# A block of feed-forward, attention and feed-forward on one core: the score banks are taken in an order fixed per head, out of turn at two units

## The chip, the cores and the metric

One Trainium2 chip, of which the kernel uses one core. The metric is the device time of one execution in microseconds (us), here the median of the runs.

## The reference, cut to what matters

```python
x = x + 0.5 * ffn(layernorm(x))
x = x + attention(layernorm(x))
x = x + 0.5 * ffn(layernorm(x))

def attention(x):                      # x: (2, 2048, 512), 16 heads of 32
    q, k, v = (proj(w_q), proj(w_k), proj(w_v))
    scores = einsum('bhqd,bhkd->bhqk', q, k) * SCALE
    probs = softmax(scores, axis=-1)
    attn = einsum('bhqk,bhkd->bhqd', probs, v)
    return einsum('bsd,ed->bse', attn, w_o)
```

All of it is float32. The change lies in the middle line alone, in `scores` and the exponential of the softmax.

## The kernel before

The program has three stages: the first feed-forward with the projections for q, k and v, the attention, and the output projection with the second feed-forward. The attention runs over 32 heads (16 heads of each of the two batch items, `NH`), numbered H = 0 to 31. A head has 16 key tiles of 128 keys (`KT`), and each key tile meets 4 chunks of 512 queries (`QC`), so a head has 64 units (`UNITS`) of 128 keys by 512 queries. Unit i of a head is chunk i mod 4 of key tile i div 4.

For each unit TensorE makes one score matmul (`scores`, line 903) into one of three PSUM banks (`s_ps`, `SR` = 3). ScalarE takes the exponential out of that bank (`scalar_tile`, line 891) and counts it in the semaphore `exp_done`. Behind each score matmul TensorE makes one matmul of the next head's maxima (`maxima`, line 907) into one of four other banks, which VectorE reduces (line 836). So that no score overwrites a bank that ScalarE has still to read, TensorE waits ahead of every score matmul for the exponential of the unit that used the bank last. The banks are taken in rotation over all units of all heads, so this is always the unit three before, and 64 units being no multiple of three, the rotation starts on another bank in each head.

TensorE's order is written out by hand in `tensor_group`. A group is two key tiles, so eight units: score, maximum, score, maximum, sixteen matmuls in all, and then the sixteen matmuls with v of the two key tiles of the group before (`out_tile`, line 934). Groups are numbered u = 0 to 7 here. After group 3 come the matmuls of the row sums (lines 950 and 958), after group 6 a transpose (line 926) of the next head's maxima, which VectorE and two DMAs carry into `att_q` ahead of the next head's first score. ScalarE also copies the output of the head before out of PSUM, between the exponentials of units 9 and 10 (line 286), and the row sums before unit 32. In the last two heads the output projection is worked in: TensorE's line 382, GpSimd's 353 and 357, ScalarE's 366. GpSimd and DMAs add up the exponentials of a head; eight tiles of them (`prob`, `PR` = 8) are kept, and ScalarE waits for the oldest to come free (`tile_free`).

Of the kernel before, what the change touches and what calls it, by code (L numbers as in the profile page):

```python
# [7 lines left out]
ACT = mybir.ActivationFunctionType  # L8
AX = mybir.AxisListType

P = 128
# [5 lines left out]
CH = 512  # L17
# [4 lines left out]
QC = SEQ // CH  # L22
# [13 lines left out]
def f32(ap):  # L36
    return ap.bitcast(F32)
# [142 lines left out]
class Stream:  # L180
# [11 lines left out]
    def load(self, sp, N, src):  # L192
        sp.dma_start(self.x[N % 2][:], chunk(src, N % NCH)).then_inc(self.loaded[N % 2], 16)
# [455 lines left out]
            st.norm.tensor(pe, self.PE_AT[t], N + 1)  # L649


NB = 3
KQ, KM = 3 * HD, 3 * HD + 2
LEAD, G = 4, 2
NG = KT // G
PR = 8
SR, MR = 3, 4
UNITS = KT * QC
AHEAD = LEAD * QC
SUMS_AFTER = 3  # L660
SUMS_AT, TURN_AT = QC * G * (SUMS_AFTER + 1), QC * 7 * G
SLOTS = UNITS + 2
CHAINS = 2
# [5 lines left out]
def sums_after(H):  # L669

    return SUMS_AFTER if H < NH - 1 else SUMS_AFTER - 1
# [6 lines left out]
def slot(p):  # L678

    return p + (p >= SUMS_AT) + (p >= TURN_AT)  # L680


SUMS_SLOT, TURN_SLOT = SUMS_AT, TURN_AT + 1
AT_SLOT = {slot(p): p for p in range(UNITS)}


def m_bank(H, at):
    return (SLOTS * H + at) % MR


def pooled(H):
    return (0, 2, 4) if H == NH - 1 else tuple(range(0, KT, 2)) + ((KT - 1,) if H < NH - 2 else ())
# [15 lines left out]
def moves_to(H, kt):  # L708

    i = moved(H).index(kt)  # L710
    return sum(len(moved(h)[i % CHAINS::CHAINS]) for h in range(H)) + i // CHAINS + 1
# [10 lines left out]
class Attention:  # L722
# [3 lines left out]
    def __init__(self, c, qk_parts, v_scr, head_out, ident, ones_sum):  # L726
# [11 lines left out]
        self.m_ps, self.s_ps, self.o_ps = c.bank[0:4], c.bank[4:7], c.bank[7]  # L738
        self.loaded = [c.sem(f"att_loaded{i}") for i in range(NB)]
        self.ones_set = c.sem("att_ones_set")  # L740
# [16 lines left out]
    def load(self, sp, X):  # L757
        b, row, col = X % NB, X % HEADS * HD, X // HEADS * SEQ
        for which, st in ((0, self.q_st[b]), (1, self.k_st[b])):
# [6 lines left out]
    def max_rows(self, sp, H):  # L766
        for r, rows in enumerate((self.neg_hi, self.neg_lo)):
            sp.wait_ge(self.neg_dve, NEG * H + 2 + r)
            sp.dma_start(f32(self.q_st[H % NB][KQ + r:KQ + r + 1, :].rearrange("o (t p) -> o t p", p=P)),
                         f32(rows[:])).then_inc(self.neg_loaded, 16)  # L770

    def head_free(self, sp, H):

        sp.wait_ge(self.s_ready, UNITS * H)
        sp.wait_ge(self.p_used, KT * H)
# [6 lines left out]
    def add(self, pool, H, kt):  # L782
        i = pooled(H).index(kt)
        pool.wait_ge(self.exp_done, UNITS * H + QC * (kt + 1))
        if i == 1:
# [8 lines left out]
    def move(self, pool, H, kt):  # L794
        x = moved(H).index(kt) % CHAINS
        into = self.dma_acc[H % 2][x]
        pool.wait_ge(self.exp_done, UNITS * H + QC * (kt + 1))
        if moves_to(H, kt) > 1:
# [42 lines left out]
    def first_block(self, dve, n):  # L841
        self.reduce_block(dve, n, self.first_bank(n), n // UNITS, n % UNITS // QC, n % QC)

# [14 lines left out]
    def vector_tile(self, dve, H, kt):  # L858
        T = H + 1 + (kt + LEAD) // KT
        for q in range(QC):  # L860
            p = QC * kt + q
            if T < NH:
                self.reduce_block(dve, UNITS * (H + 1) + AHEAD + p, self.m_ps[m_bank(H, slot(p))], T % 2, (kt + LEAD) % KT, q)
            if kt == TURN - 1 and q == 0 and H + 1 < NH:
# [19 lines left out]
    def scalar_tile(self, act, H, kt):  # L884
        self.tile_free(act, H, kt)
        if H > 0 and kt == G * (sums_after(H) + 1):
            act.wait_ge(self.t_ready, H)
            self.head_out.copy_sums(act, H - 1, self.sums_bank(H - 1))
        for q in range(QC):
            act.wait_ge(self.s_ready, UNITS * H + QC * kt + q + 1)  # L890
            self.nc.scalar.activation(self.prob[kt % PR][:, q * CH:(q + 1) * CH], self.s_ps[(UNITS * H + kt * QC + q) % SR][:], ACT.Exp,  # L891
                                      scale=SCALE).then_inc(self.exp_done, 1)
            if q == 1 and H > 0 and kt == G:
                act.wait_ge(self.p_used, KT * H)
                self.head_out.copy_out(act, H - 1, self.o_ps)
# [1 line left out]


    def scores(self, pe, H, kt, q):
        i = UNITS * H + kt * QC + q  # L900
        if i >= SR:
            pe.wait_ge(self.exp_done, i - SR + 1)
        self.nc.tensor.matmul(self.s_ps[i % SR][:], self.k_st[H % NB][0:KM, kt * P:(kt + 1) * P],  # L903
                              self.q_st[H % NB][0:KM, q * CH:(q + 1) * CH], start=True, stop=True).then_inc(self.s_ready, 1)

    def maxima(self, m, T, qt, q):
        self.nc.tensor.matmul(m[:], self.q_st[T % NB][0:KQ, qt * P:(qt + 1) * P], self.k_st[T % NB][0:KQ, q * CH:(q + 1) * CH],  # L907
                              start=True, stop=True).then_inc(self.m_ready, 1)
# [53 lines left out]
    def bank_free(self, pe, H, at):  # L962
# [8 lines left out]
        elif old < 0:  # L971
            pe.wait_ge(self.m_read, UNITS * (H + 1) + AHEAD + old + 1)
        else:
            pe.wait_ge(self.m_read, min(UNITS * (H + 1) + AHEAD + AT_SLOT[old] + 1, UNITS * NH))

# [418 lines left out]
```

## Time and profile before

| | us |
|---|---|
| median of 3 runs | 2977.56 (2976.84 to 2978.41) |
| the profiled execution | 2976.84 |
| its span in the profile | 2975.0 |
| TensorE busy in it | 2898.6 |
| VectorE, ScalarE, GpSimd busy | 2051.4, 1603.5, 1383.1 |

The first score matmul of head 0 begins at 818.0 us of the span and the last of head 31 at 2404.6 us. Rows are named by the engine (PE is TensorE's matmul, PEld its weight load, DVE VectorE, ACT ScalarE, POOL GpSimd) and by the line of the kernel. A matmul's row is longer than the matmul's share of the engine, since matmuls are pipelined: what counts is from the start of one to the start of the next.

### The profile page before, as it was taken

The numbers are of one execution on the slowest core, as the hardware profiler recorded it, in microseconds if no ns is written. First come the engines' busy times: TensorE is split into PE (matmuls) and PEld (weight loads), VectorE is DVE, ScalarE is ACT, GpSimd is POOL, SyncE is SP. The second block draws the span as 40 slices with busy tenths as digits, with TensorE's granted clock in tenths as the row PEclk, the third lists the DMA queues.
The fourth block names the chain that finished last, engine by engine and source line by source line (L and its number), as shares of the span: only waits on it lengthen the run. The fifth ranks groups of instructions, "written<-read, shape, count | busy, mean of one in ns | idle before, by whom it ended". The sixth has DMA issues, their size and how long they took to land.

```text
span 2975.0 us, 38468 instructions
## 1 busy us (share of the span) xinstructions
PE 2898.6 (97%) x14528; PEld 1939.1 (65%) x14528; DVE 2051.4 (69%) x3050; ACT 1603.5 (54%) x2851; POOL 1383.1 (46%) x522
## 2 busy tenths in 40 slices
PE   6999998999999999999999999999999899999999
PEld 5888887887755555555555555555555457888887
DVE  5555555767787787878787878788888355555553
ACT  5444434332276666666666666666666553343333
POOL 0000000000089898988898889898888720000000
PEclk9999999999999999999999999999999999999999
DMA  4110002555389999998999999999898872222200
GB/s 154 59 57 29 29 29 62 199 192 177 124 219 205 220 209 224 203 231 198 228 203 233 200 229 202 229 204 229 204 229 207 220 196 69 57 57 57 57 29 29
DMA packets 189275, 459.97 MB, mean 155 GB/s; under 512 B 90273, under 2 KB 91297, under 8 KB 148769
## 3 DMA queue, kind: packets, MB, share of 16 engines
q0 software_dynamic: 36720, 267.40, 39.0%
q1 hardware_dynamic: 152368, 190.11, 22.6%
q8 instruction: 114, 1.87, 0.3%
q14 instruction: 73, 0.59, 0.1%
HBM read 121.91 MB, written 67.63 MB: 64 GB/s over the span
## 4 chain that ended last, share of the span: by engine, by line
PE 88%; DVE 4%; DMA 3%; ACT 3%; POOL 1%; issue 1%; SPq 0%; ACTq 0%; DVEq 0%; POOLq 0%
PE bank L903 16%; PE bank L511 16%; PE bank L530 15%; PE bank L934 15%; PE bank L907 14%; PE bank L642 8%; PE bank L382 3%; ACT att_p L891 2%; DMA att_q<-att_neg_lo 1%; DVE att_row_max L836 1%; PE bank L958 1%; PE bank L950 1%; DVE norm_inv L109 1%; DVE norm_work L119 1%; POOL att_acc L792 1%
## 5 line engine op out<-in xcount | busy, mean ns | idle before, releaser
L836 DVE TENSOR_REDUCE att_row_max<-bank 128x1 f32<-128x512 f32 x2048 | 1255.2, 681 | 318.0 <-PE bank L907 318.0
L891 ACT ACTIVATE att_p<-bank 128x512 f32<-128x512 f32 x2048 | 1035.5, 627 | 414.3 <-PE bank L903 408.5
L792 POOL TENSOR_TENSOR att_acc<-att_acc,att_p 128x2048 f32<-128x2048 f32 x217 | 1066.6, 4915 | 32.8 <-ACT att_p L891 28.2
L903 PE MATMUL bank<-att_q,att_k 98*128 98x512 f32 x2048 | 848.5, 415 | 18.2 <-ACT att_p L891 11.2
L907 PE MATMUL bank<-att_k,att_q 96*128 96x512 f32 x2048 | 808.1, 396 | 10.8 <-DVE att_row_max L836 10.6
L903 PEld LDWEIGHTS bank<-att_q,att_k 98*128 98x128 f32 x2048 | 384.4, 188 | 396.7 <-issue 202.4
L934 PE MATMUL bank<-att_p,att_v 128*32 128x512 f32 x4096 | 497.1, 603 | 0.0
L443 DVE TENSOR_TENSOR ffn_hid_lo<-ffn_hid,ffn_hid_hi 128x512 fp32r<-128x512 f32 x256 | 176.0, 688 | 420.8 <-ACT ffn_hid_hi L486 402.5
L483 ACT ACTIVATE ffn_hid<-bank,up_s 128x512 f32<-128x512 f32 x256 | 176.1, 688 | 488.0 <-PE bank L511 487.2
L907 PEld LDWEIGHTS bank<-att_k,att_q 96*128 96x128 f32 x2048 | 389.6, 190 | 60.6 <-DVE att_row_max L836 13.3
L511 PE MATMUL bank<-hi,ffn_up_w 128*128 128x512 f32 x1024 | 401.0, 392 | 13.6 <-DVE lo L123 13.6
L530 PE MATMUL bank<-ffn_hid_hi,ffn_down_w 128*128 128x512 f32 x1024 | 399.6, 390 | 1.9 <-DVE ffn_hid_lo L443 1.9
L511 PE MATMUL bank<-lo,ffn_up_w 128*128 128x512 f32 x1024 | 400.7, 391 | 0.0
L530 PE MATMUL bank<-ffn_hid_lo,ffn_down_w 128*128 128x512 f32 x1024 | 399.7, 390 | 0.0
L780 POOL MEMSET att_k<- 2x2048 f32 x3 | 5.4, 1805 | 814.8 <-PE bank L530 501.7
L807 POOL DMA_DIRECT2D att_dma_acc<-att_p x161 | 203.8, 1266 | 139.4 <-DMA att_dma_acc<-att_p 97.8
L934 PEld LDWEIGHTS bank<-att_p,att_v 128*32 128x32 f32 x4096 | 107.5, 109 | 242.8 <-ACT att_p L891 158.5
L511 PEld LDWEIGHTS bank<-hi,ffn_up_w 128*128 128x128 f32 x1024 | 193.6, 189 | 56.1 <-issue 15.2
L530 PEld LDWEIGHTS bank<-ffn_hid_hi,ffn_down_w 128*128 128x128 f32 x1024 | 192.7, 188 | 42.9 <-DVE ffn_hid_lo L443 2.4
L511 PEld LDWEIGHTS bank<-lo,ffn_up_w 128*128 128x128 f32 x1024 | 193.6, 189 | 40.8
L530 PEld LDWEIGHTS bank<-ffn_hid_lo,ffn_down_w 128*128 128x128 f32 x1024 | 192.7, 188 | 40.5
L486 ACT ACTIVATE ffn_hid_hi<-bank,up_s 128x512 fp32r<-128x512 f32 x256 | 174.6, 682 | 0.0
(104 smaller groups left out, 2236.8 us busy)
## 6 DMA issues: line engine op xcount, KB each, us to landing
att_dma_acc<-att_p POOLq DMA_DIRECT2D x225, 1024.0 KB, 8.9
att_dma_acc<-att_dma_acc POOLq DMA_DIRECT2D x30, 1024.0 KB, 12.6
x<-x_after_ffn SPq DMA_DIRECT2D x16, 1024.0 KB, 7.6
att_q<-q_hi SPq DMA_DIRECT2D x64, 256.0 KB, 4.0
att_k<-k_hi SPq DMA_DIRECT2D x64, 256.0 KB, 10.0
x_after_ffn<-x_out SPq DMA_DIRECT2D x8, 1024.0 KB, 9.4
q_hi<-qkv_o_hi SPq DMA_DIRECT2D x32, 256.0 KB, 2.0
q_lo<-qkv_o_lo SPq DMA_DIRECT2D x32, 256.0 KB, 2.4
```

What stands on the lines that cost most here:

```text
L443: nc.vector.tensor_tensor(self.hid_lo[:, ht % RING, :], self.hid[:, ht % RAW, :], f32(self.hid_hi[:, ht % RING, :]), ALU.subtract).then_in ...
L483: nc.scalar.activation(self.hid[:, ht % RAW, :], self.up_ps[ht % 2][:], ACT.Relu, scale=self.vecs["up"][:, ht:ht + 1])
L511: ins = nc.tensor.matmul(self.up_ps[ht % 2][:], signs.up[:, ht // 4, dt, ht % 4 * P:(ht % 4 + 1) * P], part[N % 2][:, dt, :], start=(dt == ...
L530: ins = nc.tensor.matmul(self.down_ps[dt][:], signs.down[:, h, dt * P:(dt + 1) * P], part[:, h % RING, :], start=(h == 0 and i == 0), stop ...
L642: ins = self.nc.tensor.matmul(self.out_ps[t % QR][:], left, right, start=(dt == 0 and (a, b) == (0, 0)), stop=(dt == DT - 1 and (a, b) == ...
L792: self.nc.gpsimd.tensor_tensor(self.acc[H % 2][:], a[:], self.prob[kt % PR][:], ALU.add).then_inc(self.summed, 1)
L807: self.nc.gpsimd.dma_start(into[:], self.prob[kt % PR][:], accum_op=ALU.add).then_inc(self.dma_summed[x], 16)
L836: self.nc.vector.tensor_reduce(self.row_max[odd][:, qt, q:q + 1], m[:], axis=AX.X, op=ALU.max).then_inc(self.m_read, 1)
L891: self.nc.scalar.activation(self.prob[kt % PR][:, q * CH:(q + 1) * CH], self.s_ps[(UNITS * H + kt * QC + q) % SR][:], ACT.Exp, scale=SCALE ...
L903: self.nc.tensor.matmul(self.s_ps[i % SR][:], self.k_st[H % NB][0:KM, kt * P:(kt + 1) * P], self.q_st[H % NB][0:KM, q * CH:(q + 1) * CH], ...
L907: self.nc.tensor.matmul(m[:], self.q_st[T % NB][0:KQ, qt * P:(qt + 1) * P], self.k_st[T % NB][0:KQ, q * CH:(q + 1) * CH], start=True, stop ...
L934: ins = self.nc.tensor.matmul(self.o_ps[rows, :], self.v_st[H % NB][:, kt, :], self.prob[kt % PR][:, q * CH:(q + 1) * CH], start=(kt == 0) ...
```

## The change

A new function works out, once for all heads, which of the three banks each of the 64 units of a head takes, and how many exponentials of the head must be done before its score may be written. In rotation each unit takes the bank that has been out of use longest. At units 23 and 46 the unit takes the second oldest instead. With these two, 64 units end on the same order of banks with which they began, so every head begins on bank 0 of the three.

What TensorE waits for ahead of a score matmul is changed by this at four units of each head, and at no other:

| unit | exponential waited for, before | after |
|---|---|---|
| 23 (last of group 2) | 20 | 21 |
| 24 (first of group 3) | 21 | 20 |
| 46 (seventh of group 5) | 43 | 44 |
| 47 (last of group 5) | 44 | 43 |

No instruction is added or removed.

```diff
+def bank_order(units, banks, second):
+
+    ages, bank = list(range(banks)), []
+    for i in range(units):
+        b = ages.pop(1 if i in second else 0)
+        ages.append(b)
+        bank.append(b)
+    assert ages == list(range(banks))
+    last = {b: u - units for u, b in enumerate(bank)}
+    freed = []
+    for i, b in enumerate(bank):
+        freed.append(last[b] + 1)
+        last[b] = i
+    return bank, freed
+
+
 NB = 3
...
 UNITS = KT * QC
+S_BANK, S_FREED = bank_order(UNITS, SR, (23, 46))
 AHEAD = LEAD * QC
...
         for q in range(QC):
             act.wait_ge(self.s_ready, UNITS * H + QC * kt + q + 1)
-            self.nc.scalar.activation(self.prob[kt % PR][:, q * CH:(q + 1) * CH], self.s_ps[(UNITS * H + kt * QC + q) % SR][:], ACT.Exp,
+            self.nc.scalar.activation(self.prob[kt % PR][:, q * CH:(q + 1) * CH], self.s_ps[S_BANK[kt * QC + q]][:], ACT.Exp,
                                       scale=SCALE).then_inc(self.exp_done, 1)
...
     def scores(self, pe, H, kt, q):
-        i = UNITS * H + kt * QC + q
-        if i >= SR:
-            pe.wait_ge(self.exp_done, i - SR + 1)
-        self.nc.tensor.matmul(self.s_ps[i % SR][:], self.k_st[H % NB][0:KM, kt * P:(kt + 1) * P],
+        i = kt * QC + q
+        if UNITS * H + S_FREED[i] > 0:
+            pe.wait_ge(self.exp_done, UNITS * H + S_FREED[i])
+        self.nc.tensor.matmul(self.s_ps[S_BANK[i]][:], self.k_st[H % NB][0:KM, kt * P:(kt + 1) * P],
                               self.q_st[H % NB][0:KM, q * CH:(q + 1) * CH], start=True, stop=True).then_inc(self.s_ready, 1)
```

## Rows read from the trace of the kernel before

**Rows 1.** The page: busy time of each engine, and two of the costliest groups.

```profile
PE 2898.6 (97%) x14528; PEld 1939.1 (65%) x14528; DVE 2051.4 (69%) x3050; ACT 1603.5 (54%) x2851; POOL 1383.1 (46%) x522
...
L891 ACT ACTIVATE att_p<-bank 128x512 f32<-128x512 f32 x2048 | 1035.5, 627 | 414.3 <-PE bank L903 408.5
...
L903 PE MATMUL bank<-att_q,att_k 98*128 98x512 f32 x2048 | 848.5, 415 | 18.2 <-ACT att_p L891 11.2
```

**Rows 2.** Windows, head 14: length, each engine's busy time, clock, DMA share.

```profile
core 0: us, PE busy (x) PEld busy (x) DVE busy (x) ACT busy (x) POOL busy (x), PEclk, DMA share, GB/s
1503.85:1553.03 49.18, 49.02 (x273) 26.42 (x273) 39.69 (x68) 33.18 (x66) 44.29 (x17) 1.00 0.95 220
```

**Rows 3.** Waits of TensorE, 915 to 2580 us: us in total, times, longest.

```profile
PE bank L903 <- ACT att_p L891: 9.4, 7, 6.2
...
PE bank L903 <- DMA att_q<-att_neg_lo: 2.9, 5, 1.0
```

**Rows 4.** Timeline of TensorE's matmuls, head 13, group 2, units 16, 22, 23, then 24.

```profile
1466.57 0.50 PE L903 MATMUL bank<-att_q,att_k 98*128 98x512 f32 x1
...
1469.48 0.39 PE L903 MATMUL bank<-att_q,att_k 98*128 98x512 f32 x1
...
1469.94 0.40 PE L903 MATMUL bank<-att_q,att_k 98*128 98x512 f32 x1
...
1470.51 1.92 PE L934 MATMUL bank<-att_p,att_v 128*32 128x512 f32 x16
1472.37 0.50 PE L903 MATMUL bank<-att_q,att_k 98*128 98x512 f32 x1
```

**Rows 5.** Timeline of the weight loads, same group, for the score of unit 23.

```profile
1469.79 0.19 PEld L903 LDWEIGHTS bank<-att_q,att_k 98*128 98x128 f32 x1
```

**Rows 6.** Timeline of ScalarE, same group, the exponentials of units 20 and 21.

```profile
1469.11 0.63 ACT L891 ACTIVATE att_p<-bank 128x512 f32<-128x512 f32 x1
...
1469.59 0.64 ACT L891 ACTIVATE att_p<-bank 128x512 f32<-128x512 f32 x1
```

**Rows 7.** Timeline, head 13, group 1: unit 8, the copy, exponential 10, weights of 13.

```profile
1460.34 0.50 PE L903 MATMUL bank<-att_q,att_k 98*128 98x512 f32 x1
...
1461.93 0.60 ACT L286 ACTIVATE head_raw<-bank 128x512 f32<-128x512 f32 x1
...
1462.41 0.62 ACT L891 ACTIVATE att_p<-bank 128x512 f32<-128x512 f32 x1
...
1463.07 0.19 PEld L903 LDWEIGHTS bank<-att_q,att_k 98*128 98x128 f32 x1 [0.56 <-ACT att_p L891]
```

**Rows 8.** Timeline, head 13, group 5: exponential 44, score of unit 46, weights of 47.

```profile
1488.32 0.63 ACT L891 ACTIVATE att_p<-bank 128x512 f32<-128x512 f32 x1
...
1488.69 0.39 PE L903 MATMUL bank<-att_q,att_k 98*128 98x512 f32 x1
...
1489.00 0.19 PEld L903 LDWEIGHTS bank<-att_q,att_k 98*128 98x128 f32 x1
```

**Rows 9.** Timeline of TensorE, the first scores of heads 15, 16, 17 and 18.

```profile
1553.04 0.50 PE L903 MATMUL bank<-att_q,att_k 98*128 98x512 f32 x1
...
1601.96 0.50 PE L903 MATMUL bank<-att_q,att_k 98*128 98x512 f32 x1
...
1650.90 0.50 PE L903 MATMUL bank<-att_q,att_k 98*128 98x512 f32 x1
...
1699.83 0.50 PE L903 MATMUL bank<-att_q,att_k 98*128 98x512 f32 x1
```

**Rows 10.** Timeline: score 47 of head 30; exponentials 20 and 21 and score 23 of head 31.

```profile
2328.87 0.79 PE L903 MATMUL bank<-att_q,att_k 98*128 98x512 f32 x1 [6.18 <-ACT att_p L891]
...
2362.87 1.09 ACT L891 ACTIVATE att_p<-bank 128x512 f32<-128x512 f32 x2 [0.16 <-PE bank L903]
...
2363.99 0.40 PE L903 MATMUL bank<-att_q,att_k 98*128 98x512 f32 x1
```

## The prediction, made before the changed kernel was run

> **What bounds the kernel now.** I read the page first. TensorE is busy 2898.6 of 2975.0 us, and the score matmul waits for almost nothing: 18.2 us in 2048 of them, 11.2 of it for ScalarE [rows 1]. The exponentials, on the other hand, are idle 408.5 us because no score is ready for them [rows 1]. So in sum ScalarE looks like an engine with time to spare. The windows view of one head says the same: in 49.18 us TensorE is busy 49.02, ScalarE 33.18, VectorE 39.69 and GpSimd 44.29, and the granted clock is 1.00 [rows 2]. The waits view of the whole attention leaves TensorE's matmuls 9.4 us on ScalarE in 7 waits, 6.2 of it one wait, and 2.9 us on the DMA of the maxima [rows 3]. TensorE sets the pace, and anything that stops it is paid in full unless a later wait of TensorE gets shorter by it.
>
> The reader is to see next that a share of 54% says nothing of one moment. I went to the timeline of a group. Score 22 begins at 1469.48 and score 23 at 1469.94, 0.46 us apart, with one maximum between them, so a matmul takes 0.23 us of TensorE [rows 4]. An exponential takes ScalarE 0.49 us: the ones of units 20 and 21 end at 1469.11 + 0.63 = 1469.74 and 1469.59 + 0.64 = 1470.23 [rows 6]. Within the eight units ScalarE is thus the slower one. It falls behind by about 0.03 us a unit and catches up only while TensorE makes the sixteen matmuls with v, 1.9 us from 1470.51 to 1472.37 [rows 4].
>
> Now the wait that the change moves. The weights of score 23 are loaded from 1469.79 [rows 5], 0.05 us after exponential 20 has ended at 1469.74 [rows 6]. That is the semaphore arriving: the wait stands ahead of the weight load, and the load starts the moment it is met. The load lies beside the maximum that is running, and the score begins at 1469.94, 0.15 us behind the start of its load, with nothing lost [rows 4, 5]. So distance three is exactly enough, with next to no room.
>
> **The change part by part.** (a) Unit 23, wait for exponential 21 in place of 20. It ends at 1470.23 [rows 6]; add 0.05 for the semaphore, and the load starts at 1470.28, 0.49 later than now. TensorE then has nothing running, so the matmul cannot hide its load. What this adds I take from the first score of a group, which also starts from an idle array: its row is 0.50 long where others are 0.40 or 0.39 [rows 4], so about 0.10 to 0.11 us pass before it runs. Score 23 then runs from 1470.39 in place of 1469.94: a stall of 0.45 us.
>
> (b) Unit 46, wait for exponential 44 in place of 43. Exponential 44 ends at 1488.32 + 0.63 = 1488.95; the load follows at 1489.00, which is just where the load of score 47 stands now, since that one waits for the same exponential [rows 8]. The score runs from 1489.11 in place of 1488.69 [rows 8]: a stall of 0.42 us. Score 47 needs only exponential 43 now and follows at the pace of the matmuls, 0.46 behind.
>
> (c) Units 24 and 47, waits loosened. Unit 24 starts at 1472.37, and the exponential 21 that it awaits ended at 1470.23 [rows 4, 6], so it had over 2 us of room, and loosening it gives nothing. Unit 47 pays no stall now, so its looser wait gives nothing beyond keeping (b) from being paid twice.
>
> (d) The order of banks itself. Heads 15, 16 and 17 begin on each of the three banks in turn, and they last 48.92, 48.94 and 48.93 us [rows 9]. Which bank a head begins on is worth at most 0.02 us, 0.6 us over all heads. I count it as nothing.
>
> Is there a case in this trace of TensorE meeting a late ScalarE in the same place? There is. In group 1 of every head but the first ScalarE slips in a copy of another bank between exponentials 9 and 10. Exponential 10 then starts at 1462.41 and ends at 1463.03, and the load of score 13 waits for it, at 1463.07 with 0.56 idle ahead of it [rows 7]. Group 1 lasts from 1460.34 to 1466.57, 6.23 us [rows 4, 7], where group 2 lasts 1466.57 to 1472.37, 5.80 us [rows 4]. A delay of ScalarE of one exponential costs TensorE 0.43 us there, and it is not given back. That is between my 0.42 and 0.45.
>
> What does the stall delay further? Behind the waiting score on TensorE's queue stand its maximum and the matmuls with v of the group before; all move by 0.45. VectorE reads the maxima more slowly than they come, so its own end moves by less. ScalarE gets exponential 23 a little later and rests sooner. GpSimd is at 44.29 of 49.18 us in a head [rows 2] and gains room. The stalls stand in groups 2 and 5, ahead of the transpose after group 6 from which the maxima travel to the next head, so that chain starts later by the same amount and hides nothing.
>
> The sum: in heads 0 to 29, 30 x (0.45 + 0.42) = 26.1 us. In head 30 unit 47 now stands 6.18 us waiting for exponential 44, which is late for another reason [rows 10]. After the change unit 46 waits for it instead, and its pair of matmuls comes behind the wait and not ahead of it, 0.46 us; with unit 23, 0.9. In head 31 there are no maxima and TensorE is slower than ScalarE in group 2: exponential 21 ends at 2362.87 + 1.09 = 2363.96, so score 23 would run from 2363.96 + 0.05 + 0.11 = 2364.12 in place of 2363.99, 0.13 us [rows 10]. Unit 46 there I put between nothing and 0.42, say 0.2. Together 27.3 us. Against the span of 2975.0 that is 3002.3, and 3004.1 for the profiled execution's own 2976.84. The median of the runs is 0.72 above that execution, so I forecast 3004.9, 0.92% slower.
>
> The bounds of a stall: at least what is left when TensorE could start as the weights begin to load, 0.45 - 0.11 = 0.34 and 0.42 - 0.11 = 0.31; at most the whole exponential, 0.49. Over 62 stalls that is 20 to 30 us.
>
> One rule of the Trainium skill would move this. Its page "TensorE: Matmul & The Clock Gate", in "The mechanism" of Part 3, says that TensorE has a reorder window of 64 and pulls a weight load ahead of matmuls in flight when it goes to the background weight buffer. If it also pulled the load of score 23 ahead of the unmet wait, the load would be done already and the lower bound would be the price. The trace here shows loads beside running matmuls, but the load of score 23 starting only 0.05 us behind the exponential that it waits for [rows 5, 6]. I give it a small chance below.
>
> **The rivals.** First, loads ahead of the wait: stalls of 0.34 and 0.31, so 30 x 0.65 = 19.5, with the last two heads 20.3; time 2998. Against it stands the 0.05 us [rows 5, 6].
>
> Second, the stalls cost nothing that lasts, and the kernel is not slower: 2977.6. The mechanism would be the start of a head. The next head's first score waits for the DMA that brings the negated maxima, and DMAs are busy 0.95 of head 14 [rows 2]. If the landing of that DMA, and not TensorE, set each head's start, and if it came when the transfers had bandwidth rather than when they were issued, a stall of 0.87 per head would be swallowed. It decides where TensorE waits for the DMA by at least 0.87 us in nearly every head. For it speaks that there are such waits; against it that they are 2.9 us in 5 heads of 32, the longest 1.0 [rows 3]. So it can swallow 3 us at most, not 27.
>
> Third, half: only one of the two stalls is paid, above all because in group 5 the freed unit 47 gives back what 46 lost. Now score 47 starts 0.46 behind score 46 with two matmuls of 0.23 between, so there is no slack to give back; but if there were, 2977.6 + 14 = 2992.
>
> Fourth, more: the shift puts other work on the path. If in every second head the maxima's DMA came 0.5 us late for TensorE, where it is late now in 5 heads [rows 3], that is 8 us on top: 3013. GpSimd's and the DMAs' load per us falls when a head gets longer, which speaks against it.
>
> **How the numbers follow.** Both stalls in full 0.74; loads ahead of the wait 0.07; nothing lasts 0.04; half 0.05; more 0.10. The forecast is that of the first, 3004.9. The range reaches down to the lower bound of the stalls, 2997, and up to 3010, the upper bound of 30 us with a little of the fourth; the second, the half and most of the fourth, 0.04 + 0.05 + 0.09, lie outside. What a measurement of this kernel tells from no change is about 0.2%, 6 us. Slower by more than that: all but the second, 0.95. Within it 0.04, faster 0.01: I see no wait that the change shortens.
>
> **What would show it.** In the changed kernel's trace, in the group with unit 23, the load of its score should stand 0.05 us behind the end of exponential 21 with some 0.3 us of idle time ahead of it, put down to ScalarE; the group should last 6.25 in place of 5.80 us, group 5 likewise 0.42 more, and heads 15 to 17 some 49.8 in place of 48.93. The wait of the weight loads on ScalarE should grow by about 62 entries. The first group to move if I am wrong is group 2: if its length stays 5.80, the step that failed is that the wait holds the weight load. If the groups grow and the heads do not, it is the second rival.

## The result and the profile after

The changed kernel takes 3002.58 us (median of 5 runs, 2997.48 to 3006.79) against 2977.56 us for the kernel before. The ratio is 1.0081, with a 95% interval of 1.0066 to 1.0096: slower by 20 to 29 us. The forecast was 3004.9, in a range of 2997 to 3010.

The page of the changed kernel. The line numbers have moved by 17: the score matmul is line 920, the exponential 908, the maxima 924, the matmuls with v 951.

```profile
span 2999.0 us, 38468 instructions
...
PE 2918.1 (97%) x14528; PEld 1936.4 (65%) x14528; DVE 2051.5 (68%) x3050; ACT 1610.4 (54%) x2851; POOL 1381.3 (46%) x522
...
L908 ACT ACTIVATE att_p<-bank 128x512 f32<-128x512 f32 x2048 | 1042.3, 624 | 437.6 <-PE bank L920 431.3
...
L920 PE MATMUL bank<-att_q,att_k 98*128 98x512 f32 x2048 | 856.3, 420 | 25.9 <-ACT att_p L908 17.8
```

No instruction has come or gone, and the shares are as before; ScalarE even stands idle longer for want of scores, 431.3 us against 408.5 [rows 1]. The page would not tell where 24 us of span went. The waits of TensorE in the attention of the changed kernel say a little more (waiting line, what it waited for, us in total, times, longest); first the matmuls, then the weight loads:

```profile
PE bank L920 <- ACT att_p L908: 15.7, 43, 6.1
...
PE bank L920 <- DMA att_q<-att_neg_lo: 0.5, 1, 0.5
...
PEld bank L920 <- ACT att_p L908: 110.8, 334, 6.6
```

Seven waits of matmuls on ScalarE have become 43 [rows 3], still only 15.7 us, because the time between two matmul rows is partly covered by the length that a row is given. The weight loads show it better: 334 waits, where the kernel before has 278:

```profile
PEld bank L903 <- ACT att_p L891: 77.7, 278, 6.6
```

The timeline of group 2 of head 13 shows the stall itself. First the matmuls:

```profile
1478.35 0.50 PE L920 MATMUL bank<-att_q,att_k 98*128 98x512 f32 x1
...
1481.27 0.39 PE L920 MATMUL bank<-att_q,att_k 98*128 98x512 f32 x1
1481.50 0.39 PE L924 MATMUL bank<-att_k,att_q 96*128 96x512 f32 x1
1482.06 0.50 PE L920 MATMUL bank<-att_q,att_k 98*128 98x512 f32 x1 [0.18 <-ACT att_p L908]
1482.40 0.40 PE L924 MATMUL bank<-att_k,att_q 96*128 96x512 f32 x1
1482.74 1.92 PE L951 MATMUL bank<-att_p,att_v 128*32 128x512 f32 x16
1484.59 0.50 PE L920 MATMUL bank<-att_q,att_k 98*128 98x512 f32 x1
```

and beside them ScalarE's exponential 21, and the weight loads of the maximum of 22 and of score 23:

```profile
1481.37 0.64 ACT L908 ACTIVATE att_p<-bank 128x512 f32<-128x512 f32 x1
```

```profile
1481.27 0.19 PEld L924 LDWEIGHTS bank<-att_k,att_q 96*128 96x128 f32 x1
1482.06 0.19 PEld L920 LDWEIGHTS bank<-att_q,att_k 98*128 98x128 f32 x1 [0.61 <-ACT att_p L908]
```

Exponential 21 ends at 1481.37 + 0.64 = 1482.01. The load of score 23 follows at 1482.06, 0.05 behind. In the kernel before the load of this unit lay 0.05 behind exponential 20 and beside the running maximum [rows 5, 6]; here it has 0.61 us of idle time ahead of it, and the matmul begins with it, as a row of 0.50; the next matmul follows 0.34 behind and not 0.23. Group 2 lasts 1478.35 to 1484.59, 6.24 us, where it lasted 5.80 [rows 4].

The same in group 5, weight loads of units 46 and 47 (with the maximum of 46 between):

```profile
1501.23 0.19 PEld L920 LDWEIGHTS bank<-att_q,att_k 98*128 98x128 f32 x1 [0.58 <-ACT att_p L908]
1501.34 0.19 PEld L924 LDWEIGHTS bank<-att_k,att_q 96*128 96x128 f32 x1
1501.57 0.19 PEld L920 LDWEIGHTS bank<-att_q,att_k 98*128 98x128 f32 x1
```

The load of 46 waits. The load of 47, which in the kernel before lay at its gate [rows 8], waits for nothing now. The group lasts 1498.00 to 1504.22, 6.22 us. And the first scores of heads 15, 16 and 17:

```profile
1566.14 0.50 PE L920 MATMUL bank<-att_q,att_k 98*128 98x512 f32 x1
...
1615.95 0.50 PE L920 MATMUL bank<-att_q,att_k 98*128 98x512 f32 x1
...
1665.75 0.50 PE L920 MATMUL bank<-att_q,att_k 98*128 98x512 f32 x1
```

A head takes 49.81 and 49.80 us, against 48.92 to 48.94 [rows 9]: 0.87 more, where the two groups have 0.44 and 0.42.

### The profile page after: what moved, and what is told of

Same layout as the page of the kernel before. It is cut to its first block, busy times and chain, and to the rows that moved or that the text cites. A ratio compares the mean times of both kernels' runs of the same rounds, so it can differ in the third digit from the quotient of the medians.

```text
span 2999.0 us, 38468 instructions
## 1 busy us (share of the span) xinstructions
PE 2918.1 (97%) x14528; PEld 1936.4 (65%) x14528; DVE 2051.5 (68%) x3050; ACT 1610.4 (54%) x2851; POOL 1381.3 (46%) x522
## 4 chain that ended last, share of the span: by engine, by line
PE 85%; ACT 8%; DVE 3%; DMA 1%; issue 1%; POOL 0%; ACTq 0%; SPq 0%; DVEq 0%; POOLq 0%
PE bank L951 16%; PE bank L511 15%; PE bank L530 15%; PE bank L920 15%; PE bank L924 11%; PE bank L642 7%; ACT att_p L908 7%; PE bank L382 3%; PE bank L975 1%; PE bank L967 1%; DMA att_dma_acc<-att_p 1%; DVE norm_inv L109 1%; ACT head_raw L286 0%; DVE norm_work L119 0%; PE bank L176 0%
## 5 line engine op out<-in xcount | busy, mean ns | idle before, releaser
L908 ACT ACTIVATE att_p<-bank 128x512 f32<-128x512 f32 x2048 | 1042.3, 624 | 437.6 <-PE bank L920 431.3
L809 POOL TENSOR_TENSOR att_acc<-att_acc,att_p 128x2048 f32<-128x2048 f32 x217 | 1049.6, 4837 | 46.1 <-ACT att_p L908 41.4
L824 POOL DMA_DIRECT2D att_dma_acc<-att_p x161 | 193.9, 1204 | 144.9 <-DMA att_dma_acc<-att_p 89.0
```

The source lines that it names most:

```text
L809: self.nc.gpsimd.tensor_tensor(self.acc[H % 2][:], a[:], self.prob[kt % PR][:], ALU.add).then_inc(self.summed, 1)
L824: self.nc.gpsimd.dma_start(into[:], self.prob[kt % PR][:], accum_op=ALU.add).then_inc(self.dma_summed[x], 16)
```

## The experiments

Seven kernels were run. The first four were compared with the kernel before on one chip (its median there 2978.93 us of 19 runs), the last three in a second comparison (2979.4 us of 9 runs).

**Each unit alone.** Two kernels in which the banks keep rotating over all heads and one unit of each head is out of turn. Against the changed kernel, cut to two places (`bank_order` here takes a test for the unit and does not ask that the order closes):

```diff
-S_BANK, S_FREED = bank_order(UNITS, SR, (23, 46))
+S_BANK, S_FREED = bank_order(UNITS * NH, SR, lambda i: i % UNITS == 23)
...
-        i = kt * QC + q
+        i = UNITS * H + kt * QC + q
```

The second kernel has 46 in place of 23.

> Out of turn at unit 23 alone, so the banks go on rotating from head to head as before. Theory (the moved wait holds the weight load of the score): group 2 of a full head grows by 0.44 us, all other groups stay, and the time grows by half of the change, 13.6 us (0.46%). Rival (the time comes from the order of banks being the same in every head): no change, since here it is not the same in every head.

> Out of turn at unit 46 alone. Theory: group 5 grows by 0.42 us, nothing else, and the time by 13.7 us (0.46%). Rival (unit 47, freed, gives part back, so that most of the loss is unit 23's): group 5 grows by under 0.2 us and the time by under 6 us.

Unit 23 alone: 2989.41 us, ratio 1.0037 (1.0025 to 1.0049). Unit 46 alone: 2988.78 us, ratio 1.0037 (1.0025 to 1.0050). By the ratio each is about 11 us, with intervals of 7 to 15 us that hold the 13.6 and 13.7 expected. From the first score of head 0 to the last of head 31 the two take 14.3 and 14.0 us more than the kernel before; what keeps the medians lower is the part behind the last score, which is 4.6 and 4.9 us shorter in these two profiles (see the total, below). Group 2 of head 13 with unit 23 alone, its first score and that of the group behind:

```profile
1474.16 0.50 PE L918 MATMUL bank<-att_q,att_k 98*128 98x512 f32 x1
...
1480.39 0.50 PE L918 MATMUL bank<-att_q,att_k 98*128 98x512 f32 x1
```

and group 5 of head 13 with unit 46 alone:

```profile
1491.30 0.50 PE L918 MATMUL bank<-att_q,att_k 98*128 98x512 f32 x1
...
1497.51 0.50 PE L918 MATMUL bank<-att_q,att_k 98*128 98x512 f32 x1
```

6.23 and 6.21 us. The stalls are there in the size forecast, they need no fixed order of banks, and in the attention the two add up to 28.3 us, where the change has 29.6. The freed unit 47 gives nothing back.

**The order of banks without the tight waits.** The same function, other units:

```diff
-S_BANK, S_FREED = bank_order(UNITS, SR, (23, 46))
+S_BANK, S_FREED = bank_order(UNITS, SR, (24, 32))
```

> The same fixed order for every head and two units out of turn, but units 24 and 32, the first of a group, where the exponential awaited has been done for over 1.6 us. Theory: groups as long as before, time within 0.1% of before. Rival (a unit out of turn, or each head beginning on the same bank, costs something by itself): the time grows as with the change, up to 25 us.

2977.79 us, ratio 0.9993 (0.9984 to 1.0003). Heads 16 and 17 begin at

```profile
1606.73 0.50 PE L920 MATMUL bank<-att_q,att_k 98*128 98x512 f32 x1
...
1655.71 0.50 PE L920 MATMUL bank<-att_q,att_k 98*128 98x512 f32 x1
```

and head 16 lasts 48.98 us, 0.04 more than before [rows 9]. The kernel with the early copy (below), whose banks rotate as before, has about as much a head outside its group 1, so this is not the order of banks. Beginning every head on one bank costs nothing that shows in the time, and neither does going out of turn, if the unit has room. The change's loss lies in where the two units stand.

**Eight stalls a head.** With the rotating banks of the two kernels above:

```diff
+S_BANK, S_FREED = bank_order(UNITS * NH, SR, lambda i: i % 8 == 7)
```

> Out of turn at the last unit of all eight groups. Theory: the stall is 0.49 + 0.16 us less the distance at which the score now follows the exponential three before: 0.44 in most groups and 0.49 to 0.5 in groups 1 and 4, where ScalarE is already late by a copy; 3.6 us a head, about 112 us in all (3090). Rival (a stall is swallowed by a later wait once there are many, as at the next head's start): clearly less, below 80 us.

3079.13 us in one run, 100 us above the median of before on that chip, where 112 were expected. Heads 16 and 17 begin at

```profile
1656.15 0.50 PE L918 MATMUL bank<-att_q,att_k 98*128 98x512 f32 x1
...
1708.51 0.50 PE L918 MATMUL bank<-att_q,att_k 98*128 98x512 f32 x1
```

52.36 us, 3.43 more than before. Taken from the first score of one group to that of the next, the median head has 0.44 more in groups 0, 2, 3 and 5, 0.49 in groups 1 and 4, where ScalarE is late by a copy already, 0.43 in group 7, and 0.25 in group 6. Group 6 is the largest miss, about 0.19 x 31 = 6 of the 12 us that are lacking. Behind its last maximum comes the transpose, which in the kernel before waits for VectorE. The last maximum and the transpose of group 6, first in the kernel before (head 13), then here (head 16):

```profile
1495.19 0.39 PE L907 MATMUL bank<-att_k,att_q 96*128 96x512 f32 x1
1495.61 0.28 PE L926 MATMUL bank<-ident,att_neg_max 128*16 128x128 f32 x1
```

```profile
1699.99 0.39 PE L922 MATMUL bank<-att_k,att_q 96*128 96x512 f32 x1
1700.23 0.27 PE L941 MATMUL bank<-ident,att_neg_max 128*16 128x128 f32 x1
```

They are 0.42 us apart before and 0.24 here: a stall of 0.44 just ahead gives VectorE the time, the later wait of 0.18 is gone, and about 0.25 is left. So a stall ahead of a wait that is there anyway is partly swallowed by it. In all other groups eight stalls are paid as fully as two, and the second rival is out.

**The size of a stall.** Out of turn earlier in the group:

```diff
+S_BANK, S_FREED = bank_order(UNITS * NH, SR, lambda i: i % UNITS in (19, 43))
```

> Out of turn at the fourth unit of groups 2 and 5 (units 19 and 43) in place of the eighth and seventh, where the score now follows the exponential three before by 0.29 us and not by 0.20 or 0.23. Theory: stall of 0.49 + 0.16 - 0.29 = 0.36 us at that unit; ScalarE, starved for a moment, comes out less late, so nothing is added further on: groups 2 and 5 grow by 0.36 each, 22 us in all, 3000. Rival (a stall out of turn always costs a whole exponential or a fixed amount): 0.42 to 0.49 each as in the change.

Group 2 of head 13 runs from the first to the second of these scores:

```profile
1476.61 0.50 PE L918 MATMUL bank<-att_q,att_k 98*128 98x512 f32 x1
...
1482.77 0.50 PE L918 MATMUL bank<-att_q,att_k 98*128 98x512 f32 x1
```

6.16 us, 0.36 more than before, as expected; the median over the heads is 0.36 for both groups. The one run took 3001.56 us, 22 above the median of before. That this is the very sum expected is luck: the attention grew by 17.6 us only, since group 3 of head 31 is 4.1 shorter, and the part behind the last score grew by 6.0. Heads 0 to 29 grew by 21.6, which is 30 x 0.72. The price is neither fixed nor a whole exponential: it is the exponential's 0.49 less the room that the score has at that place (unit 19 begins 0.29 us after exponential 16 has ended, and 0.05 to the load and 0.11 more, 0.16, is the least, so its room is 0.13).

**A matmul put into the wait.** The changed kernel, with the maximum of units 23 and 46 ahead of the score:

```diff
             for q in range(QC):
-                self.scores(pe, H, kt, q)
+                late = QC * kt + q in (23, 46)
+                if not late:
+                    self.scores(pe, H, kt, q)
                 if T < NH:
...
+                if late:
+                    self.scores(pe, H, kt, q)
```

> The changed kernel, with the maximum of units 23 and 46 put ahead of the score on TensorE's queue, so that a matmul of 0.23 us that needs no exponential fills part of the wait. Theory: each stall falls by 0.23 us, groups 2 and 5 grow by 0.21 and 0.19 us over before in place of 0.44 and 0.42, and the kernel is 12 us slower than before, not 25. Rival (a fixed price of the wait, or of restarting TensorE): no different from the change, 25 us.

2994.69 us, ratio 1.0052 (1.0039 to 1.0066), so 15 us slower than before (12 to 20) and not 25, where 12 were expected. Heads 0 to 29 grew by 12.1. The weight loads around unit 23 (maximum of 22, maximum of 23, score 23), and the first scores of groups 2 and 3 of head 13:

```profile
1478.09 0.19 PEld L924 LDWEIGHTS bank<-att_k,att_q 96*128 96x128 f32 x1
1478.48 0.19 PEld L924 LDWEIGHTS bank<-att_k,att_q 96*128 96x128 f32 x1 [0.21 <-DVE att_row_max L853]
1478.89 0.19 PEld L920 LDWEIGHTS bank<-att_q,att_k 98*128 98x128 f32 x1 [0.22 <-ACT att_p L908]
```

```profile
1475.17 0.50 PE L920 MATMUL bank<-att_q,att_k 98*128 98x512 f32 x1
...
1481.18 0.50 PE L920 MATMUL bank<-att_q,att_k 98*128 98x512 f32 x1
```

The group lasts 6.01 us, 0.21 more than before. The idle time ahead of the load of score 23 falls from 0.61 to 0.22 us. Work that does not need the exponential shortens the stall by its own length, so the stall is a wait and not a fixed price of restarting; what is fixed in it is the 0.11 us by which a load that begins together with its matmul makes the next one later.

**The other way: less delay on ScalarE.** The stall of group 1, which served the prediction as a measure, is in the kernel before too. It comes from a copy on ScalarE. Here the copy is moved in the kernel before, and nothing of the change is in it:

```diff
     def scalar_tile(self, act, H, kt):
...
+        if H > 0 and kt == G:
+            act.wait_ge(self.p_used, KT * H)
+            self.head_out.copy_out(act, H - 1, self.o_ps)
         for q in range(QC):
...
-            if q == 1 and H > 0 and kt == G:
-                act.wait_ge(self.p_used, KT * H)
-                self.head_out.copy_out(act, H - 1, self.o_ps)
```

> The kernel before, its banks in rotation, with ScalarE's copy of the head output moved from between exponentials 9 and 10 to ahead of exponential 8, where ScalarE is idle. Nothing else is changed. Theory (any delay of ScalarE inside a group beyond some 0.05 us is paid by TensorE through the same wait): exponential 8 is then late by 0.15 us and not exponential 10 by 0.49, so group 1 shrinks by about 0.3 us from 6.23, 9 to 10 us in all, 2968, 0.3% faster. Rival (the extra 0.43 us of group 1 has another cause): no change; or, if the copy's own wait for the last output matmuls is late, group 1 grows.

2968.42 us (2966.43 to 2971.86), ratio 0.9962 (0.9948 to 0.9976): 11 us faster than the kernel before, the only version that beats it. ScalarE and the first scores of groups 1 and 2 of head 13:

```profile
1456.19 0.67 ACT L894 ACTIVATE att_p<-bank 128x512 f32<-128x512 f32 x1
1458.30 0.60 ACT L286 ACTIVATE head_raw<-bank 128x512 f32<-128x512 f32 x1 [1.44 <-PE bank L934]
1458.80 4.02 ACT L894 ACTIVATE att_p<-bank 128x512 f32<-128x512 f32 x8
```

```profile
1458.03 0.50 PE L903 MATMUL bank<-att_q,att_k 98*128 98x512 f32 x1
...
1463.91 0.50 PE L903 MATMUL bank<-att_q,att_k 98*128 98x512 f32 x1
```

The copy now falls into ScalarE's pause, 1.44 us after the last exponential of the group before (number 7), and group 1 takes 5.88 us where it took 6.23 [rows 4, 7]. The median head is shorter by 0.35 in that group and by nothing in the others. It is the same wait as the change's, read with the other sign.

## Why the prediction was right

**The wait holds the weight load.** Right, and the step on which all else hung. In the changed kernel the load stands 0.05 us behind the exponential now awaited. The first rival, loads pulled ahead of the wait, would have made group 2 grow by 0.34; it grew by 0.44. One of the signs named was off: 0.3 us of idle time ahead of that load, where it has 0.61. The rows of the kernel before had it, since the load ahead of it there ends at 1469.48 + 0.19 = 1469.67 and 1470.28 - 1469.67 = 0.61:

```profile
1469.48 0.19 PEld L907 LDWEIGHTS bank<-att_k,att_q 96*128 96x128 f32 x1
```

No term of the sum rests on it. The loads have 56 more waits, where 62 were named.

**The sizes.** Forecast 0.45 and 0.42. Over the heads the median group 2 grew by 0.44 and group 5 by 0.42. Summed over all heads, groups 2 and 5 grew by 13.7 us each, 27.4 together, against 27.3 in the sum. The 0.11 in each came out, but its reason was put loosely: the first score of a group does not start from an idle array, as the matmuls with v ahead of it run to 1470.51 + 1.92 = 1472.43 and it begins at 1472.37 [rows 4]. What it shares with score 23 of the changed kernel is that its load begins no earlier than the matmul:

```profile
1472.36 0.19 PEld L903 LDWEIGHTS bank<-att_q,att_k 98*128 98x128 f32 x1 [0.84 <-issue]
```

**Loosened waits and the order of banks count for nothing.** Right: 0.9993 with the same order and slack units.

**Nothing swallows it.** Nearly right, and the last heads were sized too low. From the first score of head 0 to the last of head 31 the changed kernel takes 29.6 us more. Heads 0 to 29 have 25.1 of it (forecast 26.1), head 30 has 1.4 (0.9) and head 31 has 3.1 (0.33). The waits on the DMA at the start of a head fell from 2.9 us in 5 heads [rows 3] to 0.5 in one, a gain of the size that the second rival was allowed; but of the kernel with slack units, which has no stalls, heads 2, 6, 13 and 19 are shorter too, by 0.3 to 1.0 us, so this gain is not shown to be the stalls'. What grew beside the stalls is time at the lower of TensorE's two clock levels. In head 1 both kernels stand for 1.5 us ahead of unit 39, and behind this stop the changed kernel, but not the one before, is granted 0.50 from 896.5 to 899.9 us; group 4 of this head is 1.6 longer. And head 31 from its first score to its last (length, busy times, clock, DMA share, GB/s), before and after:

```profile
2345.57:2404.63 59.06, 52.41 (x260) 23.43 (x256) 25.43 (x18) 35.63 (x67) 28.19 (x14) 0.91 0.91 226
```

```profile
2372.54:2434.72 62.18, 55.30 (x260) 24.11 (x256) 28.57 (x19) 35.86 (x67) 30.75 (x14) 0.86 0.90 225
```

The sum had nothing for the clock.

**The total.** The span grew by 24.0 us and the median by 25.0, against 27.3 forecast, and that they are so near is in part luck: the attention took 2.3 more than the sum, and the part behind the last score took 6.1 less, 564.28 us in the profiled execution of the changed kernel and 570.37 in that of the kernel before, though the change has nothing there. In the kernel before TensorE stands there for the VectorE work that leads to the first matmul of the feed-forward, and it runs twice for 3.4 us at the lower clock level, once behind this stop and once behind a second:

```profile
2417.60 0.47 PE L511 MATMUL bank<-hi,ffn_up_w 128*128 128x512 f32 x1 [2.89 <-DVE lo L123]
...
2489.56 0.62 PE L530 MATMUL bank<-ffn_hid_hi,ffn_down_w 128*128 128x512 f32 x1 [1.93 <-DVE ffn_hid_lo L443]
```

```profile
2418.10:2421.50 3.40, 3.40 (x9) 2.59 (x8) 0.49 (x1) 2.01 (x3) 0.00 (x0) 0.50 1.01 376
2489.80:2493.20 3.40, 3.40 (x9) 2.61 (x9) 3.40 (x3) 0.78 (x1) 0.00 (x0) 0.50 0.00 0
```

Half of 6.8 us and the 2.9 make 6.3, about the difference of 6.1. The changed kernel has neither the first stop nor a stretch at the lower level there. The kernel with the slack units, whose heads are longer by some 0.05 us only, has a first stop of 1.3 us, no such stretch, and is 4.5 us shorter as well:

```profile
2410.48:2976.30 565.82, 558.66 (x2502) 455.61 (x2501) 298.18 (x333) 222.32 (x305) 10.10 (x2) 1.00 0.21 62
```

Over the nine profiles this part takes 564.3 to 576.5 us, and where it is shortest the first stop is nothing, where it is longest 7.8 and 8.5 us (fourth unit, maxima first). So the stalls as such do not shorten it. Why the VectorE work comes sooner or later, and why the clock falls in one kernel and not in the other, stays open.

## What to carry to other kernels

A wait that is next to nothing in the waits of the matmuls can still have next to no room: measure it from the end of the instruction awaited to the start of the weight load, in the timeline, at that unit. In this kernel, with three banks and a reader (0.49 us) slower than the writer (0.46 us) within a burst, waiting for the unit three before costs nothing unless a copy delays the reader, and waiting for the one two before costs 0.36 to 0.49 us, 0.25 where a later wait takes a part. At the first unit of a group, where the reader has just rested, it costs nothing. An engine busy for 54% of the time can own the critical wait: the copy on ScalarE cost 0.35 us a head less in its pause than between two exponentials.

## What was not expected of the hardware

A stall of TensorE costs less than the idle time shown ahead of the weight load: 0.61 us ahead of the load, 0.44 in the group. In the kernel before that load has 0.12 us of idle time ahead of it (from 1469.67 to 1469.79) and loses nothing. In the row of the matmul it shows as only 0.18 us. The length of the group is the number to read. And the clock: the stop of 1.93 us for VectorE (line 443) at 2489.56 us is followed by 3.4 us at 0.50 in the kernel before. The changed kernel has the same stop in the same work, and is granted 1.00 throughout:

```profile
2515.10 0.50 PE L530 MATMUL bank<-ffn_hid_hi,ffn_down_w 128*128 128x512 f32 x1 [1.93 <-DVE ffn_hid_lo L443]
```

```profile
2480.00:2999.00 519.00, 513.14 (x2258) 423.52 (x2256) 273.04 (x313) 197.19 (x276) 0.00 (x0) 1.00 0.18 51
```

The length of a stop alone does not tell whether the clock falls behind it.
